# Four of a recommendation kernel's 416 row gathers are fetched by SyncE, one row at a time

## The reference: what is computed

```python
x = dense_inputs                                   # (2048, 13)
for W, b, g, be in bot:                            # 13 -> 512 -> 256 -> 64
    x = _bn(relu(x @ W + b), g, be)                # batch norm over the 2048 samples
embs = tbl[idx] for each of the 26 tables          # (2048, 26, 64)
T = concatenate([embs, x[:, None, :]], axis=1)     # (2048, 27, 64)
Z = einsum('bnd,bmd->bnm', T, T)                   # all pairs of the 27 vectors
R = concatenate([x, Z[:, iu, ju]], axis=1)         # upper triangle: 351 products
h = R
for W, b, g, be in top:                            # 415 -> 512 -> 256 -> 1
    h = _bn(relu(h @ W + b), g, be)
return sigmoid(h)
```

## Time and profile before

| | us |
|---|---|
| median of 3 runs (lowest to highest) | 589.19 (588.45 to 590.12) |
| span of the profiled execution | 987.2 |
| POOL busy in it | 401.1 |
| PE busy in it | 448.2 |
| DVE busy in it | 233.0 |
| ACT busy in it | 189.5 |

### The profile page before, as it was taken

One profiled execution on the slowest core, in us unless ns is written; L12 is line 12 of the kernel. 1 busy time (PEld: TensorE's weight loads), 2 busy tenths in 40 slices (PEclk: granted clock), 3 DMA queues, 4 the chain that ended last, 5 costly groups with the idle time before them and its releaser, 6 DMA issues.

```text
span 987.2 us, 13898 instructions
## 1 busy us (share of the span) xinstructions
PE 448.2 (45%) x5827; PEld 321.1 (33%) x5827; DVE 233.0 (24%) x640; ACT 189.5 (19%) x509; POOL 401.1 (41%) x426
## 2 busy tenths in 40 slices
PE   7751151624425161523517162351715244177787
PEld 3430020513214051412405051240514133165664
DVE  6600130402112040312204031220403022055542
ACT  5400020302011030302103030210303021044523
POOL 6777227072542707163361706336171634500000
PEclk9975575756657575755757575575757557577999
DMA  5122001020110202010110101011020101100000
GB/s 168 23 27 26 12 9 26 3 26 10 18 18 11 26 3 27 7 23 14 14 23 5 26 6 23 14 14 23 5 27 6 24 13 15 22 3 1 3 1 0
DMA packets 15895, 18.30 MB, mean 19 GB/s; under 512 B 7614, under 2 KB 8894, under 8 KB 15695
## 3 DMA queue, kind: packets, MB, share of 16 engines
q0 software_dynamic: 13312, 13.66, 10.6%
q1 hardware_dynamic: 2524, 3.72, 1.2%
HBM read 17.34 MB, written 0.01 MB: 18 GB/s over the span
## 4 chain that ended last, share of the span: by engine, by line
another core or an unknown queue 61%; PE 23%; ACT 10%; issue 3%; DVE 3%; DMA 0%; ACTq 0%; SPq 0%; DVEq 0%
PE l_bank L469 11%; ACT Zs L280 7%; PE l_bank L409 3%; PE l_bank L393 2%; PE l_bank L466 2%; PE l_bank L399 1%; PE l_bank L423 1%; ACT TT L636 1%; PE z_bank L455 1%; PE l_bank L507 1%; PE tr_bank L351 1%; DVE TT L853 1%; ACT hidden L582 0%; ACT hidden_hi L648 0%
## 5 line engine op out<-in xcount | busy, mean ns | idle before, releaser
L320 POOL DMA_INDIRECT emb<-table,stage x390 | 374.3, 960 | 424.1 <-DVE stage L802 309.2
L455 PE MATMUL z_bank<-TT 64*27 64x26 f32 x3840 | 127.5, 217 | 403.5 <-issue 388.4
L455 PEld LDWEIGHTS z_bank<-TT 64*27 64x27 f32 x3840 | 89.2, 132 | 442.9 <-issue 442.9
L254 DVE COPY Zs<-z_bank 27x112 f32<-27x112 f32 (+3 forms) x272 | 88.2, 324 | 498.7 <-remote 488.6
L280 ACT ACTIVATE Zs<-z_bank 27x112 f32<-27x112 f32 (+3 forms) x272 | 91.6, 337 | 552.8 <-remote 535.2
L469 PE MATMUL l_bank<-Zs,tw_sb 128*128 128x128 f32 x840 | 117.1, 298 | 0.0
L469 PEld LDWEIGHTS l_bank<-Zs,tw_sb 128*128 128x128 f32 x840 | 112.6, 215 | 0.0
L853 DVE COPY TT<-tr_bank 128x512 f32<-128x512 f32 (+1 forms) x60 | 51.1, 979 | 4.2 <-PE tr_bank L441 3.9
L351 PE MATMUL tr_bank<-idle_operand 128*128 128x512 bf16 x112 | 46.9, 590 | 0.0
L864 DVE BATCH_NORM_STATS2 stats_t<-h_block 128x128 f32 x60 | 17.7, 294 | 123.8 <-ACT hidden_hi L648 123.8
L441 PE MATMUL tr_bank<-ident,emb 128*128 128x128 f32 x195 | 30.8, 284 | 35.1 <-DVE TT L853 28.8
(11 more groups left out here) (120 smaller groups left out, 282.5 us busy)
## 6 DMA issues: line engine op xcount, KB each, us to landing
emb<-table,stage POOLq DMA_INDIRECT x416
tw_sb<-tw0x SPq DMA_DIRECT2D x1, 1792.0 KB
bw_sb<-bw SPq DMA_DIRECT2D x1, 512.0 KB
tw_sb<-tw SPq DMA_DIRECT2D x1, 512.0 KB
twx_sb<-twx SPq DMA_DIRECT2D x1, 256.0 KB
idx_raw<-idx SPq DMA_DIRECT2D x1, 169.0 KB, 3.0
bw_sb<-bw SPq DMA_DIRECT2D x2, 64.0 KB
hidden<-dense_t SPq DMA_DIRECT2D x1, 104.0 KB
```

Source lines behind the costliest of these rows:

```text
L254: last = copy(dst, src[:, :, ZC * q:ZC * q + w])
L320: pool.indirect_dma_start(out=emb[:, s, k, h, :], out_offset=None, in_=table, in_offset=bass.IndirectOffsetOnAxis(ap=stage[:, s, col:col + ...
L455: mm = nc.tensor.matmul(bank[QUAD * j:QUAD * j + V, x * ZM:(x + 1) * ZM], one, one[:, 1:V], start=True, stop=True)
```

## The change

Four of the 26 gathers of the last part, those of half 0 and pairs k = 0 to 3, are no longer issued by POOL. DVE adds the table offsets to the indices for them early on and writes 128 x 4 row numbers to a new tile, `sp_rows`. SP, after its loads, goes through the 512 row numbers: it loads one into a register and issues a DMA of that one row, 256 bytes, to a new tile, `emb_sp`. PE waits for four new semaphores (`landed_sp`) ahead of the first transposes of half 0 in the last part, and reads the first two transposes' operands from `emb_sp`. The pair k covers tables 2k and 2k+1, so these are tables 0 to 7 for one half of the part's samples.

```diff
+SP_PAIRS = 4
...
+        sp_rows = sb("sp_rows", [P, SP_PAIRS], U32)
+        emb_sp = sb("emb_sp", [P, SP_PAIRS, D])
...
+            sp.wait_ge(sp_rows_ready, 1)
+            for k in range(SP_PAIRS):
+                for p in range(P):
+                    row = sp.value_load(sp_rows[p:p + 1, k:k + 1], min_val=0, max_val=NF * VOCAB - 1)
+                    sp.dma_start(emb_sp[p:p + 1, k, :], table[bass.ds(row, 1), :]).then_inc(landed_sp[k], 16)
+
             sp.wait_ge(prob_ready, 1)
...
                     for k in range(k0, k1):
+                        if h == 0 and k < SP_PAIRS:
+                            continue
                         col = 2 * k + h
                         pool.indirect_dma_start(
...
-                pe.wait_ge(landed_last[h][g], (LAST_GROUPS[g][1] - LAST_GROUPS[g][0]) * 16)
+                k0, k1 = LAST_GROUPS[g]
+                by_sp = max(0, min(SP_PAIRS, k1) - k0) if h == 0 else 0
+                for k in range(k0, k0 + by_sp):
+                    pe.wait_ge(landed_sp[k], P * 16)
+                if k1 - k0 > by_sp:
+                    pe.wait_ge(landed_last[h][g], (k1 - k0 - by_sp) * 16)
                 for c, (k, k_end) in enumerate(last_blocks(g)):
+                    source = emb_sp if h == 0 and k < SP_PAIRS else emb_last[:, h, :, :]
                     tr = nc.tensor.transpose(last_tr_bank[g][0:(k_end - k) * D, c * P:(c + 1) * P],
-                                             emb_last[:, h, k:k_end, :].rearrange("p k d -> p (k d)"),
+                                             source[:, k:k_end, :].rearrange("p k d -> p (k d)"),
                                              ident[:, :])
...
             nc.vector.memset(idx_clamped[:, PARTS * PW:(PARTS + SLOTS) * PW], 0.0).then_inc(consts_ready, 1)
+            last0 = idx_clamped[:, LAST * PW:LAST * PW + 2 * SP_PAIRS].rearrange("p (k h) -> p k h", h=2)[:, :, 0]
+            base0 = table_base[:, 0:2 * SP_PAIRS].rearrange("p (k h) -> p k h", h=2)[:, :, 0]
+            nc.vector.tensor_tensor(sp_rows[:, :], last0, base0, ALU.add).then_inc(sp_rows_ready, 1)
```

More of the change, by code:

```diff
@@ L185, in rec_program @@
         landed = [[sem("landed%d_%d" % (s, g)) for g in range(GROUPS)] for s in range(SLOTS)]
+        sp_rows_ready = sem("sp_rows_ready")
+        landed_sp = [sem("landed_sp%d" % k) for k in range(SP_PAIRS)]
         landed_last = [[sem("landed_last%d_%d" % (h, g)) for g in range(len(LAST_GROUPS))] for h in range(2)]
```

## The result

| | us |
|---|---|
| before, median of 4 runs | 589.06 (588.45 to 590.12) |
| changed kernel, median of 4 runs | 732.17 (730.86 to 734.38) |
| ratio | 1.2441, 95% interval 1.2411 to 1.2471 |
| span of the changed kernel's recording | 731.1 |

The change costs 143 us. The forecast was 586.9 us, with a range from 584.2 to 703. Rival (a), SP late, came true, and went beyond its upper bound.

The account below looks back on a forecast made before the run. POOL's gather issue was taken to bound the kernel: 582.2 us summed plus 7.0 kept constant make 589.2. Four gathers fewer save 5.0, PE's path lets 2.3 through, SP's rows cost nothing: 586.9 us, range 584.2 to 703.

Parts of the forecast that it names:

- Rival (a): SP's 512 rows come late for the last part's half 0 and the kernel gets slower, 646 to 703 us; chance 0.36.
- upper bound: SP's dearest row: issue 0.61, load 0.30, register instructions at 0.10 each, 1.21 us a row, giving 703 us.
- What bounds the kernel: Without the recording's stretched pace, POOL's gathers at 1.248 us each are slower than PE and never wait for a slot.
- The sum against the time: POOL's 416 gathers, last landing and the end after half 1's transposes: 582.2 us, where the runs take 589.2.
- The 7.0 us "around and errors": Remainder between summed 582.2 and measured 589.2 us, for what lies around the span and errors, kept constant.
- Part one: POOL issues four gathers fewer in the last part, 4 x 1.248 = 5.0 us sooner.
- Part two: PE's path to half 1's last gathers lets only 2.3 of the 5.0 us through; gain between 0.8 and 3.0.
- the 30.2 us: PE's path from part 14's last transpose to the transposes of half 1's last gathers, read from the stretched recording.
- my formula: POOL's 32.4 us for the last 26 gathers against PE's path of 30.2: PE waits 2.3 us, which is the gain.
- Part three: SP's 512 rows at 0.75 us each take 384 us, done by about 391, costing nothing before half 0's transposes.
- the threshold, 0.984: Highest price in us a row at which SP's 512 rows fit their 503.8 us and cost nothing.
- The formula: Time if SP is late: 83.2 + 512 r us, with r the price of a row on SP.

Follow-up runs that it names:

- run 6: Changed kernel with one register load for four row numbers and no bound checks: 587.63 us, ratio 0.9995 to the kernel before, runs from 584.8 to 592.5.
- run 11: Half 0's four gathers by SP, one register load for four row numbers, no bound checks, timed again: 586.28 us, ratio 0.9963 to the kernel before.
- Runs 9, 11 and 12: SP fetches four gathers, four numbers per load, against the kernel before: half 1's pairs 8 to 11 1.0005 (first and last), half 0's pairs 0 to 3 0.9963 (middle).
- run 4: Changed kernel with the two bounds left out of the register load: 587.27 us, ratio 0.9963 to the kernel before.
- experiment 5: The kernel before, unchanged, recorded once more: 589.24 us, with a span of 586.7.

## Why the prediction was wrong

- **What bounds the kernel, right.** POOL's issue at 1.248 us a gather, with no wait for slots: 118.6 us between the loop's gathers, and no wait but the one for the first row numbers, in the changed kernel's recording. That the stretched pace of PE belonged to one recording was shown by a second one of the same kernel: 586.7 us instead of 987.2.
- **The sum against the time, right by luck of a constant.** The 7.0 us "around and errors" were about 2.5 around. The rest was mostly POOL: its last gather was issued at 530.3 (529.34 + 0.95), where my sum had 525.8. When I left out the waits for a slot, the 0.30 us gap that any gather has behind the one before it went with them, for 13 gathers in all, some 4 us: 377 of 389 gaps were left in the loop's 114.9 us, where the changed kernel's recording shows 118.6, and one more in the last part. The same 4.5 us made most of SP's window ending too early.
- **Part one, right.** Each gather fewer is 1.25 us of POOL.
- **Part two, right in size, in part by luck, and wrong in place.** Predicted 2.3 us; measured 2.1 and 2.2, and for half 0's four with the load of four numbers 0.6 in the scattered run 6 and 2.4 in run 11. But the cap isn't at the last gathers. PE's order has a group of half 1 ahead of half 0's layer 0, and that wait, five gathers before the last, is where POOL holds PE. I read the 30.2 us as PE's own path though a wait of this kind lies inside it, only invisible, as in that recording POOL was long done. Runs 9, 11 and 12 show it: spared gathers behind that group gained nothing. Nor is the path's length fixed: where PE waited for no gather it took 30.3 us (run 4) to 32.1 (run 6), which by my formula would be a gain of anything from 0.3 to 2.1 us.
- **Part three failed, and it is the whole result.** The term: a row's price, 0.75 us forecast, 1.21 the upper bound, 1.273 measured. By piece, forecast to measured: DMA 0.40 with its gap, 0.265 and 0.05; register load 0.20, 0.498; three register instructions 0.15, in truth four (0.152, 0.018, 0.042, 0.029), 0.24, and five more gaps, 0.22. The DMA was over-priced. The load was under-priced because it was taken from small accesses of DVE and ACT, which it turned out not to resemble; nothing in the trace of before had an engine load a number into a register. And the register instructions were priced as gaps, where each costs its own time and a gap.
- **The upper bound was no bound.** It stacked the dearest issue on a load of 0.30, for which there was no reason but the nearest row. With a load of 0.50, not excluded by anything I had, the same stack would have given 1.41 us a row and a range that held the time. I had named the threshold, 0.984, as lying inside the bounds, and still gave the side above it 0.36.
- **The formula held.** 83.2 + 512 x 1.273 = 735, measured 732. Inside it, errors cancel: half 0 took 675.50 - 660.38 = 15.1 us and not 12.7, the end 55.6 and not 54.5, the landing 1.1 and not 1.9, and some 5 us of the 7.0 weren't there. That it comes within 3 us is luck as well.
- **The page.** The section "Latency and other measured facts" of the Trainium skill's "DMA: Bandwidth & Descriptors" was on the right side, with its floor of some 600 ns. Here the median was 498 ns and the minimum 468, so the measurement decides: on SP the floor lies lower than the page's. The estimate made with it, 672 us, was 60 too low all the same, since the register instructions in it were still priced as gaps.

## What to carry to other kernels

When work is shifted to an idle engine, its hidden capacity is a number of operations: window divided by the price of one, and the price must be measured, since beyond the threshold everything missing is paid in full (here 1.273 against 0.985 us a row was 143 us lost against 2 gained). Per-item instructions of a sequencer add up with their gaps, so load several registers in one instruction and leave out what only checks. And a spared instruction is worth its time only ahead of the point where the next engine really waits: find that wait in the profile, and take the work from in front of it. The clock granted in one recording and not in another was worth 1.6 us here, so a gain of 2 us is read from the times of many runs.

## What the runs showed of the hardware

- A register load from SBUF costs SP 0.498 us for one number, 0.563 for four and 0.996 for six (medians). That it is one nearly fixed price for each four begun would fit; two, three and five weren't tried.
- SP issues one-row DMAs of 256 bytes back to back at 0.300 us each; 512 of them beside 412 gathers left POOL's 1.25 us a gather as it was.
- The two bounds given to a loaded value cost 0.29 us at each load (1.273 against 0.985 us a row).
- The same kernel's recording can span 987.2 us once and 586.7 the next time, in the first with PE's small matmuls held back only while gathers are issued. Not settled: why, and whether that execution itself took so long.
- The clock granted to PE differs between recordings at one and the same place: half 0's layer 0 took 6.10 us at 0.65 in experiment 5, 5.55 at 0.72 with constant addresses and 4.05 at 1.00 without bounds. Not settled: why.
- After 144 us of waiting, PE's first transposes took 0.43 us where those of the kernel before take 0.27; PEclk stands at 5 in the slices of the wait, the lower of the clock's two levels, 1.2 GHz.
